# Moving the sigma(q) sum of an attention layer behind that of sigma(k) on VectorE

## The reference

```python
def step(carry, inp):
    mem, z = carry
    q_s, k_s, v_s = inp
    sq = jax.nn.elu(q_s) + 1.0
    att_mem = sq @ mem / (sq @ z)
    sk = jax.nn.elu(k_s) + 1.0
    mem = mem + jnp.einsum('bhlk,bhlv->bhkv', sk, v_s)
    z = z + sk.sum(axis=-2, keepdims=True).transpose(0, 1, 3, 2)
    att_dot = jax.nn.softmax(jnp.einsum('bhik,bhjk->bhij', q_s, k_s) * scale, axis=-1)
    att = att_dot @ v_s
    att = gate * att_mem + (1.0 - gate) * att
    return ((mem, z), att)
# ffn: sqrt((xn @ cos(theta + theta_noise))**2 + (xn @ sin(phi + phi_noise))**2)
```

## Time and profile before

| | |
|---|---|
| median of 2 runs | 1420.45 us (1419.94 to 1420.96) |
| the profiled execution | 1420.56 us |
| its span, first to last instruction, slowest core (core 4) | 1419.0 us |
| spans of the eight cores | 1407.1 to 1419.0 us |
| mean granted TensorE clock, core 4 | 0.737 of full speed |
| busy, share of the span | TensorE 56%, VectorE 49%, ScalarE 24%, GpSimd 16% |

### The profile page before, as it was taken

One profiled execution on the slowest core, in us unless ns is written; L12 is line 12 of the kernel. 1 busy time (PEld: TensorE's weight loads), 2 busy tenths in 40 slices (PEclk: granted clock), 3 DMA queues, 4 the chain that ended last, 5 costly groups with the idle time before them and its releaser, 6 DMA issues.

```text
span 1419.0 us, 14762 instructions; the slowest of 8 cores (1407.1 to 1419.0 us)
## 1 busy us (share of the span) xinstructions
PE 792.4 (56%) x5125; PEld 423.0 (30%) x5125; DVE 692.8 (49%) x1409; ACT 336.5 (24%) x829; POOL 221.9 (16%) x127
## 2 busy tenths in 40 slices
PE   0300147476666657565766666575657666665753
PEld 0200024242423224242424242232424242423321
DVE  2000445555555655464645556565646455555540
ACT  1011312213040312222130403132221304031222
POOL 1011000203021111112030211111120302011113
PEclk9855558777786869787777768696877777686867
DMA  9656200010101010010101010100101010100001
GB/s 173 154 123 160 43 2 30 1 62 0 60 3 60 3 59 3 0 62 1 62 0 60 3 60 2 60 2 7 55 0 62 1 61 1 60 3 30 2 1 59
DMA packets 18123, 56.51 MB, mean 40 GB/s; under 512 B 1217, under 2 KB 5249, under 8 KB 18050
## 3 DMA queue, kind: packets, MB, share of 16 engines
q0 software_dynamic: 8000, 20.97, 7.2%
q1 hardware_dynamic: 10050, 34.59, 6.7%
HBM read 41.98 MB, written 16.78 MB: 41 GB/s over the span
## 4 chain that ended last, share of the span: by engine, by line
PE 40%; DVE 28%; ACT 12%; DMA 9%; issue 7%; DVEq 2%; POOL 1%; ACTq 1%; POOLq 1%
PE pb L123 11%; PE pb L492 8%; ACT e_bf L319 8%; PE pb L370 6%; DVE pT_sb L643 6%; DVE negm L614 5%; PE pb L381 4%; PE pb L393 3%; DVE xnT_sb L566 3%; DMA stage<-th 3%; DVE attT_bf L679 2%; PE pb L434 2%; PE pb L450 2%; DMA stageB<-thn 2%; DVE m2t L657 2%
## 5 line engine op out<-in xcount | busy, mean ns | idle before, releaser
L253 POOL TENSOR_TENSOR stage<-fscr 128x1024 f32<-128x1024 bf16 x32 | 62.2, 1945 | 1009.5 <-ACT fscr L138 774.5
L123 PE MATMUL pb<-sin_r,xnT_sb 128*128 128x512 bf16 x512 | 157.2, 476 | 87.7 <-ACT fscr L138 87.7
L123 PE MATMUL pb<-cos_r,xnT_sb 128*128 128x512 bf16 x512 | 157.7, 478 | 48.8 <-DVE sk_bf L596 48.8
L319 ACT ACTIVATE e_bf<-pb,negms 128x256 bf16<-128x256 f32 x256 | 117.4, 485 | 164.8 <-DVE negms L619 164.8
L492 PE MATMUL pb<-wo_r,attT_bf 128*128 128x512 bf16 x256 | 113.8, 624 | 71.4 <-DVE attT_bf L679 71.4
L643 DVE CAST pT_sb<-pb 128x512 bf16<-128x512 f32 x128 | 79.5, 683 | 128.2 <-PE pb L434 128.2
L370 PE MATMUL pb<-xnT_sb,wq_b 128*128 128x256 bf16 x512 | 93.5, 368 | 74.9 <-DVE xnT_sb L566 54.0
L307 ACT ACTIVATE scr<-scr 128x1024 f32<-128x1024 f32 x16 | 16.9, 1058 | 411.9 <-DVE scr L574 411.9
L123 PEld LDWEIGHTS pb<-sin_r,xnT_sb 128*128 128x128 bf16 x512 | 57.9, 117 | 186.8 <-issue 157.2
L420 PE MATMUL pb<-kT_bf,qT_bf 64*128 64x256 bf16 x256 | 27.1, 279 | 150.9 <-DVE v_bf L586 107.1
L138 ACT ACTIVATE fscr<-pb 128x512 bf16<-128x512 f32 x128 | 73.1, 596 | 159.2 <-PE pb L123 146.3
(11 more groups left out here) (92 smaller groups left out, 1125.4 us busy)
## 6 DMA issues: line engine op xcount, KB each, us to landing
x_sb<-x SPq DMA_DIRECT2D x16, 1024.0 KB, 5.0
y<-out_sb SPq DMA_DIRECT2D x16, 1024.0 KB, 5.2
stage<-th POOLq DMA_DIRECT2D x2, 1024.0 KB, 22.3
stageB<-th POOLq DMA_DIRECT2D x2, 1024.0 KB, 23.0
stage<-thn POOLq DMA_DIRECT2D x2, 1024.0 KB, 11.1
stageB<-thn POOLq DMA_DIRECT2D x2, 1024.0 KB, 12.3
stage<-ph POOLq DMA_DIRECT2D x2, 1024.0 KB, 7.0
stageB<-ph POOLq DMA_DIRECT2D x2, 1024.0 KB, 7.0
```

The source lines that it names most:

```text
L123: li = t_.matmul(pb[6 + half][:, :], xnT_sb[:, ppf + 256 * dt + 128 * u: ppf + 256 * dt + 128 * u + 128], w_s[:, 1024 * dt + 512 * half: 1 ...
L253: g.tensor_mul(stage[:, 0:1024], fscr[:, 0:1024], fscr[:, 0:1024])
L319: sc.activation(e1_bf[:, 2048 * u + 256 * h: 2048 * u + 256 * h + 256], sl, AF.Exp, bias=negms[:, c:c + 1], scale=0.125, accum_out=den[:, ...
```

## The change

The sum for q is taken from its place between the copies of kT_bf and v_bf, and put behind the sum for k, with its wait on s_eq and its increment of s_sq. No other instruction is changed, on any engine. Nothing is added or removed.

```diff
@@ -577,10 +577,6 @@
                 v.tensor_copy(kT_bf[:, 0:512], pb[4][:, :])
                 v.tensor_copy(kT_bf[:, 512:1024],
                               pb[5][:, :]).then_inc(s_kte, 1)
-                v.wait_ge(s_eq, t + 1)
-                v.scalar_tensor_tensor(sqT_bf[:, :], qT_bf[:, :], 0.0,
-                                       scr[:, 1024:2048], ALU.max,
-                                       ALU.add).then_inc(s_sq, 1)
                 for u in range(2):
                     v.wait_ge(s_v, 2 * t + u + 1)
                     v.tensor_copy(v_bf[:, 512 * u:512 * u + 512],
@@ -599,6 +595,10 @@
                                                     3072 + 512 * u + 512],
                                                 ALU.max, ALU.add)
                 li.then_inc(s_sk, 1)
+                v.wait_ge(s_eq, t + 1)
+                v.scalar_tensor_tensor(sqT_bf[:, :], qT_bf[:, :], 0.0,
+                                       scr[:, 1024:2048], ALU.max,
+                                       ALU.add).then_inc(s_sq, 1)
                 if t >= 1:
                     v.wait_ge(s_md, t)
                     mz3 = memz_bf[0:64, :].rearrange("p (h c) -> p h c", c=65)
```

## The result

| | before | after |
|---|---|---|
| median of all runs | 1419.4 us (30 runs) | 1430.48 us (32 runs) |
| ratio of the runs | 1 | 1.007, interval 1.0054 to 1.0085 |
| mean span of the eight cores | 1412.6 us | 1419.0 us |
| mean span of the slowest core | 1417.9 us | 1429.0 us |
| mean granted clock | 0.739 | 0.768 |

What follows compares the result with a forecast made beforehand. No engine is full; a chain of hand-overs through TensorE, ScalarE and VectorE bounds the kernel. Start of chunk 1 at 209.2, plus 1099.0 for 14 chunks, 115.0 for the rest and 1.56 around it: 1424.8 us; range 1415 to 1438.

Steps and rivals of the forecast that it cites:

- The cover at the old place: Between the copies of kT_bf and v_bf: TensorE's v projection hides the 1.13 us removed, so the gain is nothing.
- The price at the new place: Behind the sum for k, ahead of the reductions: 1.13 us more on the chain in each of chunks 1 to 15, +17.0.
- The wait before sin: TensorE's idle time ahead of the sin group: to grow from 2.60 to 3.73 us.
- Chunk 0: ScalarE's second exponential follows the first at once, 3.76 us earlier; less 1.13, a single gain of 2.6 us.
- The plain sum: Whole kernel, every delay simply added: 1420.56 - 2.6 + 17.0 = 1435.0 us; as the full-price rival, chance 0.28.
- The pace of 78.5 holds: Chunk lengths: TensorE's clock takes up the added work, chunks stay at 78.5 us; likeliest case, 1424.8 us, chance 0.42.
- 14 chunks of 78.5 = 1099.0: From the start of chunk 1: 14 chunks all at 78.5 us, the earlier short chunks lost; 1099.0 us.
- the stretch behind them: Rest of the span after the 14 chunks: 1419.0 - (211.82 + 1093.34) + 1.13 = 115.0 us.
- The rival of the longer pause: Sin group: TensorE's longer wait keeps its matmuls at 1.2 GHz, 1.7 us more in 15 chunks; 1460 us, chance 0.07.

Runs made afterwards that it cites:

- only7: The sum for q moved in chunk 7 alone, against the kernel before; 1428.54 us in one execution.
- after_fill2: The changed kernel plus extra matmuls, up to 18 per pause, in TensorE's longer pauses of chunks 1 to 15; 1301.32 us.
- only0: The sum for q moved in chunk 0 alone, against the kernel before; ratio 0.9975 (0.9966 to 0.9984).

## Why the prediction was right, and where it was off

- **The cover at the old place**: right. It was TensorE's v projection, and nothing was gained. The pause of the second copy is 1.03, not the 0.4 that I wrote: with the sum gone both copies wait, together 1.47 us. The 1.13 us of work that left had to turn up as idle time (0.43 + 1.13 = 1.56), and I had not carried it over.
- **The price at the new place**: right. 1.13 us a chunk at a steady clock; in the profile after, the reductions start 466.40 - 463.39 = 3.01 us after the sum for k, where it was 701.47 - 699.60 = 1.87, and ScalarE's wait is longer by the same 1.14. The wait before sin was to be 3.73 and is 3.91, because the cos group ahead of it ended sooner (5.13 us at a granted clock of 0.70, where it was 5.30 at 0.68). The cos group and the reductions (L614) of before, from the timeline of chunk 7:

```profile
701.13 5.30 PE L123 MATMUL pb<-cos_r,xnT_sb 128*128 128x512 bf16 x16 [3.23 <-DVE sk_bf L596]
701.47 2.46 DVE L614 TENSOR_REDUCE negm<-pb 128x2 f32<-128x512 f32 x4
```

- **Chunk 0**: 2.6 was forecast; the trace shows 2.8, and the experiment 3.5 with an interval that holds both.
- **The plain sum**, 1435: not what came (1430.5), but what comes when the clock is held: +15.4 us there against +14.4.
- **The pace of 78.5 holds**: right for the ordinary chunk (median 78.52), with the clock risen to 0.78; `only7` shows one delay taken up in this way. As a rule for the sum over the chunks it failed, as the next point says.
- **The size was off by 5.5 us**, and the step that failed is "14 chunks of 78.5 = 1099.0", taken from one core. Two things were missing. First, the mean core became longer by 1419.0 - 1412.6 = 6.4 us, where I had 4.2. The small delays in chunks 5 and 9 were answered by short chunks before, that in 13 by one of 78.27; now chunks of 80.2 to 81.6 us stand there (two or three of the chunks 6, 9, 10 and 14 on every core). Part by part, in the mean of the cores of the two profiles: the start of chunk 1 moved by -2.1 us (forecast -2.6), the 14 chunks grew from 1090.5 to 1101.5, by 11.0 (forecast 5.7), and the stretch behind them shrank by 1.3, where I had 1.13 more. This last term was wrong as well, in the other direction: by the measure that gave 115.0, core 1 has 1426.6 - 1310.16 = 116.4, but the seven others 112.0 to 112.1; why stays open. So the forecast came as near as it did partly because two errors have opposite signs. Second, the metric is the slowest core. Before, all cores fell into the same pattern from chunk 3 on, and the slowest was 1417.9 - 1412.6 = 5.3 us above the mean. After, they follow different patterns, and it is 1429.0 - 1419.0 = 10.0 above it. That adds 4.7, give or take 1: in the kernel before beside the later experiments this distance was 6.3. Together the two are 2.2 + 4.7 = 6.9 us; the forecast started from 1420.56, which is 1.2 above the median of before, and that leaves the 5.7 between 1424.8 and 1430.5. A forecast made from one core's trace could not hold this, but the rows of the cores' spans could have warned of it.
- **The rival of the longer pause** (1460): did not come. TensorE's pause grew to 3.9 us and the granted clock rose. The Trainium skill, TensorE: Matmul & The Clock Gate, section "HAM oscillation — how this bites in real kernels", has pauses throttle the clock, so that the group behind one starts at the low level. The trace agrees with that before, where the sin group started at 0.50 behind a pause of 2.60 us, and disagrees after: behind 3.91 us it starts at 1.00 and falls to 0.50 within the group. It took 5.30 us, where it was 5.16, and over the whole chunk the mean clock rose from 0.74 to 0.78. Busy time by stretch, after (core 1, chunk 3), then before (core 4, chunk 7):

```profile
473.96:474.50 0.54, 0.54 (x3) 0.29 (x4) 0.54 (x4) 0.34 (x1) 0.05 (x1) 1.00 0.00 0
475.00:477.00 2.00, 2.00 (x6) 0.69 (x5) 1.66 (x2) 0.21 (x1) 1.38 (x1) 0.50 0.00 0
```

```profile
709.04:709.60 0.56, 0.56 (x2) 0.26 (x3) 0.56 (x4) 0.34 (x1) 0.07 (x1) 0.50 0.00 0
```

- Why the preferred lengths are 78.5 and about 81.6 was not tested by a run of its own. That they hang on the clock is shown as far as this: at 1.00 the length is another (68.90 us) and follows the chain by the full 1.13. The extra matmuls also fill TensorE's pauses, so the clock was not the only thing that changed there.

## What to carry to other kernels

When TensorE's clock moves up and down inside a loop, the loop's length is not the sum of its chain: here one delay in one chunk cost nothing, and in all chunks a first delay cost 0.8 of its 1.13 us a chunk, a second of the same size 2.7. Look first whether iterations have a repeated length at a repeated clock, and price small edits with the clock held up, where a microsecond is a microsecond. Put off-chain work into a pause that the timeline shows to be longer than the work, not behind a neighbour that looks alike; and on eight cores remember that the slowest counts, so that whatever makes cores differ costs too.

## What the runs showed of the hardware

- Extra matmuls that compute nothing, 7 to 18 in each pause, made the kernel faster by 9.5% (1421.96 to 1285.91 us), by holding the granted clock at 1.00 through chunks 1 to 14 (0.75 to 0.76 before, in the mean of the 14). The Trainium skill, TensorE: Matmul & The Clock Gate, section "Part 1: The HAM clock gate", puts the cost of the warm-up at the start at under 1% of a typical kernel. Here it was ten times that, because the clock fell anew in every chunk, which that figure does not cover.
- TensorE's clock has a third level beside 0.50 and 1.00. In the profile of `after_fill2`, core 4 was granted 0.81 (busy time by stretch 405 to 485 us); its chunk 4 took 77.03 us at a mean of 0.80, where the same chunk of core 3 took 70.04 at 1.00. The profiles of the kernels before and after show the two levels alone.
- Once the cores share one pattern, their chunks are alike to a few hundredths of a microsecond: chunk 6 took 76.15 to 76.17 us on all eight cores of the kernel before, and again on all eight of `only0` (76.14 to 76.17).
